# Moving the attention kernel's value burst from behind the score burst to between the second and the third unit's transposes

## The reference, cut to what matters

```python
q, k, v = (x @ W + b for W, b in ((Wq, bq), (Wk, bk), (Wv, bv)))
scores = q @ k.T / sqrt(32) + attention_bias
scores = where(mask, -inf, scores)
ctx = softmax(scores) @ v
x = x + ctx @ Wo + bo
```

## Time and profile before

| what | us |
|---|---|
| median of 3 runs | 2548.05 (2542.47 to 2548.43) |
| the profiled execution's own time | 2545.35 |
| its span, first to last instruction | 2543.6 |
| PE busy | 2394.3 (94%) |
| DVE busy | 1355.5 (53%) |
| ACT busy | 994.5 (39%) |
| POOL busy | 983.2 (39%) |

### The profile page before, as it was taken

How to read it: one execution, slowest core, us unless ns; L and a number is a source line. 1 busy time by engine, 2 the same in 40 slices (tenths; PEclk the granted TensorE clock), 3 DMA queues, 4 the chain that set the end, 5 groups by cost and what they waited for, 6 DMA issues and landing times. The chain is left out here.

```text
span 2543.6 us, 44268 instructions
## 1 busy us (share of the span) xinstructions
PE 2394.3 (94%) x16068; PEld 1911.5 (75%) x16068; DVE 1355.5 (53%) x2713; ACT 994.5 (39%) x1985; POOL 983.2 (39%) x806
## 2 busy tenths in 40 slices
PE   5999999999995799999999999998589999999999
PEld 4788888888884577777777777776478888888887
DVE  5354554454454677776777777776433333323332
ACT  3232232232230576766676666665312111111211
POOL 0031431332331576766676666764022112202200
PEclk9999999999997899999999999999799999999999
DMA  5201101101101656564555556553501100110100
GB/s 167 76 17 58 41 27 47 41 33 41 41 27 62 214 167 188 169 202 154 185 171 181 161 179 187 166 167 113 182 17 50 50 16 33 49 49 0 49 33 17
DMA packets 133377, 243.69 MB, mean 96 GB/s; under 512 B 13228, under 2 KB 17468, under 8 KB 133200
## 3 DMA queue, kind: packets, MB, share of 16 engines
q1 hardware_dynamic: 133200, 241.39, 29.8%
HBM read 216.17 MB, written 25.20 MB: 95 GB/s over the span
## 5 line engine op out<-in xcount | busy, mean ns | idle before, releaser
L968 POOL TENSOR_TENSOR at_bias<-at_bias,at_mask 128x512 f32<-128x512 f32 x512 | 590.5, 1178 | 311.4 <-DMA at_bias<-in_fside_Bx16xSxS 273.9
L494 ACT ACTIVATE L_hid<-L_turn,L_b1c 128x512 f32<-128x512 f32 x256 | 176.4, 689 | 955.9 <-PE L_turn L290 950.8
L662 DVE CAST L_hh<-L_hid 128x512 fp32r<-128x512 f32 x256 | 122.6, 479 | 761.3 <-PE L_acc L762 721.9
L288 PE MATMUL L_turn<-L_xth,L_w1h 128*128 128x512 f32 x1024 | 404.4, 395 | 7.7 <-ACT L_hid L494 5.4
L760 PE MATMUL L_acc<-L_w2h,L_hh 128*128 128x512 f32 x1024 | 403.0, 394 | 8.5 <-DVE L_hl L664 8.5
L289 PE MATMUL L_turn<-L_xth,L_w1l 128*128 128x512 f32 x1024 | 400.5, 391 | 0.0
L290 PE MATMUL L_turn<-L_xtl,L_w1h 128*128 128x512 f32 x1024 | 400.5, 391 | 0.0
L762 PE MATMUL L_acc<-L_w2l,L_hh 128*128 128x512 f32 x1024 | 400.1, 391 | 0.0
L761 PE MATMUL L_acc<-L_w2h,L_hl 128*128 128x512 f32 x1024 | 400.1, 391 | 0.0
L999 ACT ACTIVATE at_bias<-at_bias,at_neg_top 128x512 f32<-128x512 f32 x512 | 362.9, 713 | 1.0 <-DVE at_neg_top L1122 0.9
L1122 DVE CUSTOM_DVE_ANT_0 at_bias<-at_score,at_bias 128x512 f32<-128x512 f32 x512 | 332.6, 684 | 51.1 <-PE at_score L1276 27.3
(11 more groups left out here) (209 smaller groups left out, 3031.6 us busy)
## 6 DMA issues: line engine op xcount, KB each, us to landing
at_bias<-in_fside_Bx16xSxS SPq DMA_DIRECT2D x256, 512.0 KB, 3.8
L_xin<-in_x SPq DMA_DIRECT2D x8, 1024.0 KB, 5.4
L_xres<-in_x SPq DMA_DIRECT2D x8, 1024.0 KB, 5.5
at_xin<-x_scratch SPq DMA_DIRECT2D x8, 1024.0 KB, 6.7
at_xres<-x_scratch SPq DMA_DIRECT2D x8, 1024.0 KB, 6.5
L_xin<-x_scratch SPq DMA_DIRECT2D x8, 1024.0 KB, 5.5
L_xres<-x_scratch SPq DMA_DIRECT2D x8, 1024.0 KB, 5.5
x_scratch<-L_xres SPq DMA_DIRECT2D x7, 1024.0 KB, 4.3
```

What stands on the lines that cost most here:

```text
L288: nc_mm = pe.matmul(out, ah, bh, start=i == 0, stop=False)
L494: nc.scalar.activation(hid[m % 2][:, :], turn[m % 2][:, :], func, bias=b1c[:, m:m + 1]).then_inc(h_act, 1)
L968: nc.gpsimd.tensor_tensor(tile, tile, mask[:, m % TT, :], ALU.add).then_inc(masked, 1)
```

## The change

The call of `context` in slot m moves from in front of the loop over the four units into it, in front of unit 2. All else stays: the same instructions, waits, buffers and DMAs.

```diff
                     if after:
                         scores(*after)
-                    if m:
-                        context(b, odd, m - 1, first)
-                    elif not first:
-                        context(b - 1, 1 - odd, BLOCKS - 1, False)
                     for j in range(GROUP):
+                        if j == 2 and m:
+                            context(b, odd, m - 1, first)
+                        elif j == 2 and not first:
+                            context(b - 1, 1 - odd, BLOCKS - 1, False)
                         if m == 8 and j == 1 and not last:
                             pe.wait_ge(xt_lo, b * KT + KT + 1)
                         elif m == 9 and j < 2 and not last:
```

## The result

The changed kernel takes 2617.29 us in the median of 4 executions (2611.13 to 2619.69); the kernel before, run in turn with it, 2546.35 (2542.47 to 2548.43; also 4 executions, one more than in the table above). The ratio is 1.0277, 95% interval 1.0252 to 1.0301: slower, inside the predicted range, 9 us above the predicted 2608. The profiled execution took 2619.62 us, its span is 2617.8, against 2543.6 before: +74.2 us. The last matmul of the attention stage starts at 1854.90 us, before at 1779.61, so all of it lies in that stage.

A forecast was written before the change was run, and what follows sets the result against it. PE's own sequence was taken to bound slots with a product; switches and uncovered waits cost 9.25 us a whole batch. Batches 1-6 55.5, batch 0 5.3, batch 7 0.8 gave +61.6 on 2545.35: 2608 us, range 2575 to 2635.

The forecast's parts named there:

- Switches: In 109 slots with both a product and the value burst: one more strip layout change, +0.18 us each, +20 us.
- The bank gen: Slots 1, 5, 6, 7, 11: the product waits for ACT's and DVE's reading, uncovered by the burst; +0.37 us a slot.
- normalize: DVE's L1143 waits for the later burst, delaying a copy and score reductions: +1.3 us in slots 0 and 12, +0.5 in 4.
- Slots 1 and 5: ACT's L1018 waits for L1143, so ACT frees the next slot's product late: +0.55 us more, 1.1 a slot.
- Slots 8 and 9: Slot 8 ends on DVE's queue, +0.5 us; slot 9's product starts late, +1.15 in batch 0, +0.7 taken.
- a much changed clock: Sign of being wrong: the clock is much changed; the other was dense slots staying within 0.2 us of 6.57.
- Rival 3: New idle times in slots 0 and 12, or longer slot 8, lower the clock more often: +26, 2634 us; 12%.
- Rival 2: Faster by the clock: the burst inside slot 8 shortens its transpose stretch, ending slot 9's clock falls: 2531 us; 4%.
- The give-back: Slots without a product, batches 0 and 7: the burst no longer delays unit 1's transposes, -0.7 us a plain slot, 6.3 back.

The follow-up runs named there:

- the give-back alone: Kernel before, with the value burst in front of unit 2 only in slots 1-3 of batch 0 and 9-11, 13-15 of batch 7: 2541.11 us, ratio 0.9977.
- the kernel with both: Kernel before, with four unused matmuls in slot 8 and the burst moved only in slots without a product but 8 and 12: 2529.27 us, ratio 0.9939.

## Why the prediction was right, and where its terms were off

**Switches, 0.18 a slot.** Right: P1 to C is 0.88, P3 to S 0.88, so the 0.11 that I took between 0 and 0.24 is what it costs; with T2's 0.07 it is 0.18, measured in slots 2, 10 and 14. The kernel with C behind T0 shows the price by itself, 0.18 to 0.23. The Trainium skill, "TensorEngine Tiling", Key Properties, says that a change of the tiling mode drains TensorE; the rows agree, at P to C too (0.88, where P0 to T1 takes 0.77 in the earlier trace rows). Slot 3 was missed: its T2 and T3 stand one behind the other without a quarter between them, and those eight transposes take 0.85 behind C, where they took 0.94 behind a product; that pays back what P1 to C costs, and the slot is unchanged. Why they are quicker behind C no row says.

**The bank gen, 0.37.** Right: 0.36 in the rows, and gone with T1 in front of P0 (7.15 to 6.75 in slot 6).

**normalize.** +1.3 for +1.4, +0.5 for +0.56. The rows of slot 12 follow the sum at each step: P0 2.13 for 2.12, C 4.14 for 4.12, L1143 5.29 for 5.26, the copy 5.90 for 5.88. With C in front of T1 slot 12 still has +1.0, which is the wait on gen (0.8) and the switches; the other 0.4 is DVE's queue behind L1143.

**Slots 1 and 5.** The sum was right, 1.1 for 1.08, and so were its rows (slot 5 of batch 2: L989 at 0.67 for 0.73, P0 at 2.19 for 2.24); its explanation was so only partly. I gave all of the extra 0.55 to L1018's wait for normalize. Without that wait 0.9 is left: 0.18 of switches, about 0.37 of gen, 0.31 of a lateness of ACT (L989 at 0.50 for 0.19) that the kernel before has too and that C covered. normalize's wait adds 0.17. That the size came out right is luck in part: most of the late start that I put down to the change was there before it. The row that would have told it (L989 0.51 into slot 5 of before) was in the trace; I read slot 6 alone, and took its 0.19 for all.

**Slots 8 and 9: the mis-sized term.** 8.9 predicted, 19.9 measured: these 11.0 are most of the 12.6 by which the span grew beyond my 61.6. Of the 19.9, waits and switches at full clock are 7 x (0.67 + 1.16) = 12.8 (batch 4, and six batches of the changed kernel with the four matmuls). I had 1.15 for slot 9 at full clock, which is right (P0 at 2.49 in batch 4, for 2.51), and then took 0.7 for six batches, on the view that a stretched C hides part of it; batch 2, with 0.72 for the clock after and 0.73 before, shows +1.03. And I left the clock as it was, while it fell more often and lower (before in five of seven slots 9, to 0.71 at the lowest; after in six, to 0.62). It took 9.7 us before and about 15.7 after, +6: after, slots 9 take 69.7 us against seven times 7.96, that is 14.0, before 55.2 against seven times 6.80, that is 7.6. The granted clock of the whole execution hardly shows it, 0.971 for 0.973. The last us is slot 8 of batch 0 (9.92 at full clock with the four matmuls, for 8.94), where DVE was busy 8.32 us with the same 16 operations that took 7.48 in batch 4. One of my signs of being wrong, a much changed clock, so came true for this one slot, and the range held because it was wide enough for it.

**Rival 3, by the clock, is partly true.** Its price was 26 us, and it said slots 0 and 12 or a longer slot 8. Slot 12, with 0.6 and 0.2 us of idle PE before P0 and T3, takes 7.97 or 7.98 in all of batches 0 to 6 at a clock of 1.00; slot 0 is alike in batches 2, 4 and 6. A fall in slot 9 costs up to 3 us (11.02 for 7.96), not 1.85. Rival 2 had the sign wrong: with the burst in the middle of slot 8 the clock fell in more slots 9, not in fewer; slot 8 became longer, where I had that stretch 0.7 us shorter.

**The give-back.** Batch 0's slots 1 to 3 gave 1.2 of 1.6, and slot 4 behind them cost 1.2 instead of 0.5. Slots 14 and 15 of batch 7, to the stage's last matmul, gave 2.9 for 1.7. Slots 8 to 13 gave nothing (+0.1 for -3.0): slot 12 costs 1.2, not 0.6, slot 11 gives nothing, slot 13 0.5, and slot 9, with -1.1 the largest, meets the clock. So batch 7 as a whole costs 2.8 us, where I had 0.8. Windows of slots 8 and 9 of batch 7, after:

```profile
1798.86:1804.62 5.76, 4.22 (x61) 3.00 (x60) 4.44 (x12) 4.82 (x10) 3.87 (x4) 1.00 0.82 260
1804.62:1810.19 5.57, 5.57 (x61) 4.24 (x61) 4.36 (x11) 3.32 (x10) 2.18 (x2) 0.69 0.83 289
```

With the clock at 1.00 the same slot takes 4.32 us (the give-back alone). That and slot 9 of batches 0 to 6 are the same miss: I sized the clock by one fall, and did not ask what else stands behind slot 8.

## What to carry to other kernels

A burst that waits for nobody is also a cover: before it is moved, read what is queued behind it on its own engine, how late each of those is let go, and in every kind of slot, for a lateness that is hidden shows in no list of waits. Who waits for the burst on another engine (here DVE's normalize, and the copies queued behind it) matters as much as what it waits for itself. And where a stretch of transposes is followed by dense matmuls, look at the granted clock of the dense part before costing anything in it: here four matmuls that nobody needs, put in idle time, took 10 us off, more than any order of the others that was tried.

## What the runs showed of the hardware

- The clock granted in slot 9 depends on what PE did in slot 8. In slot 8 of the kernel before PE is busy for 5.8 to 6.8 of 8.3 to 8.7 us, with 12 score matmuls, a value burst and transposes, and in five of seven slots 9 the clock then lies at 0.71 to 0.83; with four more 512-column matmuls (1.18 us) in slot 8 it was 1.00 in seven of seven, and again in the kernel with both. The Trainium skill, "TensorE: Matmul & The Clock Gate", Part 4, says that transposes don't count as busy for the clock in the way that other matmuls do; the kernels with the four matmuls agree with it, though no run put transposes in their place, and batch 0 of the changed kernel, whose slot 9 fell to 0.67 with them, shows that it is not all. Why slot 9 stayed at 1.00 in batch 4 of the changed kernel, and fell in six batches of the kernel whose slots 0, 4, 8 and 12 are as before, stays open.
- VectorE's L1147 (128x512, two inputs in SBUF) and GpSimd's adds (L968) hold each other up. In slot 8 of batch 0 L1147 took 0.75 us before and 1.53 after; its mean over 32 went from 828 to 1055 ns. The timeline of the changed kernel there has GpSimd at work over it:

```profile
924.12 2.71 POOL L968 TENSOR_TENSOR at_bias<-at_bias,at_mask 128x512 f32<-128x512 f32 x2 [2.35 <-DMA at_bias<-in_fside_Bx16xSxS]
924.29 1.53 DVE L1147 SCALAR_TENSOR_TENSOR at_ctl<-at_normal,at_bvc,at_cth 128x512 fp32r<-128x512 f32 x1
```

  Before, it began at 920.53, in a gap of GpSimd between 919.46 and 922.42. Taken over all 64 (32 in each kernel), the rows are regular. The 35 that no add touches take 0.74 or 0.75 us. Where an add is under way when L1147 starts, L1147 ends 0.55 us after the end of that add: 10 of 11 before (0.76 to 1.70 us long), 13 of 14 after (0.82 to 1.68). The eleventh meets the add's last 0.01 us and takes 0.75; the fourteenth (1.78) meets two adds and ends 0.55 after the second. Where L1147 starts first, four times after, it takes 0.75, and the add takes 1.41 to 1.52 for 1.17. The Trainium skill, "GPSIMD Engine Reference", Specifications, lists contention with VectorE instructions that have two SBUF inputs; the rows agree. No run took GpSimd's work away, but who comes second is the one that waits in each of these rows.
